# A later convolution beside a recurrent scan, and part of its loads issued by ScalarE

## The reference

```
x = x + conv(x, taps=cond) + conv_b          # per channel, causal, 128 taps over 64 steps
h = cond
for t in range(64):
    i_r, i_z, i_n = split(x[:, t] @ W_ih + b_ih)
    h_r, h_z, h_n = split(h @ W_hh + b_hh)
    r, z = sigmoid(i_r + h_r), sigmoid(i_z + h_z)
    n = tanh(i_n + r * h_n)
    h = (1 - z) * n + z * h
    out[:, t] = x[:, t] + h
```

## Time and profile before

| | |
|---|---|
| timed runs, median of 3 | 1212.7 us (1211.54 to 1214.32) |
| the profiled execution | 1213.68 us, of which 1211.9 us are the span of its instructions |
| PE busy | 1179.8 us, 97% of the span |
| DVE, ACT busy | 558.5 us (46%), 466.6 us (39%) |
| DMA packets | 251906, of these 176810 under 512 bytes |
| mean granted clock of TensorE | 0.995 of full speed |

### The profile page before, as it was taken

How to read it: one execution, slowest core, us unless ns; L and a number is a source line. 1 busy time by engine, 2 the same in 40 slices (tenths; PEclk the granted TensorE clock), 3 DMA queues, 4 the chain that set the end, 5 groups by cost and what they waited for, 6 DMA issues and landing times.

```text
span 1211.9 us, 14952 instructions
## 1 busy us (share of the span) xinstructions
PE 1179.8 (97%) x5524; PEld 977.4 (81%) x5524; DVE 558.5 (46%) x942; ACT 466.6 (39%) x804; POOL 15.0 (1%) x20
## 2 busy tenths in 40 slices
PE   5989999989999999999999999999999999999997
PEld 4968878878888888888888888888888888888886
DVE  3737768766874434334333343333433334333333
ACT  4346656656663333233332333332333323333232
POOL 0300000000000000000000000000000000000000
PEclk9989999999999999999999999999999999999999
DMA  9978888788842011110111101111011110011100
GB/s 260 284 144 165 164 171 170 160 171 178 165 124 70 20 34 35 35 35 20 32 35 35 35 21 31 35 35 35 22 30 35 35 35 24 28 35 35 35 18 18
DMA packets 251906, 92.18 MB, mean 76 GB/s; under 512 B 176810, under 2 KB 246442, under 8 KB 249824
## 3 DMA queue, kind: packets, MB, share of 16 engines
q1 hardware_dynamic: 248332, 90.52, 32.3%
q10 hardware_dynamic: 3540, 1.22, 0.4%
HBM read 57.56 MB, written 34.14 MB: 76 GB/s over the span
## 4 chain that ended last, share of the span: by engine, by line
PE 91%; SPq 3%; DMA 3%; DVE 1%; ACT 1%; issue 0%; ACTq 0%; DVEq 0%
PE bank L818 82%; PE bank L841 3%; PE bank L807 2%; PE bank L773 2%; SPq L361 1%; DMA xres<-stage 1%; PE bank L842 1%; DMA early<-early_result 1%; SPq L372 1%; PE bank L794 1%; SPq L346 1%; DMA conv_b_rows<-in_L_cond_b_dram 0%; DMA x_unit<-in_x_dram 0%; SPq L417 0%; DMA h<-in_cond_dram 0%
## 5 line engine op out<-in xcount | busy, mean ns | idle before, releaser
L818 PE MATMUL bank<-w_ih_hi,xT_hi 128*128 128x512 f32 x768 | 309.2, 403 | 1.7 <-ACT bank L546 1.7
L818 PE MATMUL bank<-w_hh_hi,hT_hi 128*128 128x512 f32 x768 | 304.4, 396 | 0.0
L818 PE MATMUL bank<-w_hh_hi,hT_lo 128*128 128x512 f32 x768 | 300.6, 391 | 0.0
L818 PE MATMUL bank<-w_hh_lo,hT_hi 128*128 128x512 f32 x768 | 300.4, 391 | 0.0
L818 PE MATMUL bank<-w_ih_hi,xT_lo 128*128 128x512 f32 x768 | 300.3, 391 | 0.0
L818 PE MATMUL bank<-w_ih_lo,xT_hi 128*128 128x512 f32 x768 | 299.5, 390 | 0.0
L818 PEld LDWEIGHTS bank<-w_hh_hi,hT_lo 128*128 128x128 f32 x768 | 144.9, 189 | 31.3
L818 PEld LDWEIGHTS bank<-w_ih_hi,xT_lo 128*128 128x128 f32 x768 | 144.2, 188 | 31.8
L818 PEld LDWEIGHTS bank<-w_ih_hi,xT_hi 128*128 128x128 f32 x768 | 144.4, 188 | 28.8 <-ACT bank L546 1.5
L818 PEld LDWEIGHTS bank<-w_hh_lo,hT_hi 128*128 128x128 f32 x768 | 145.0, 189 | 28.0
L818 PEld LDWEIGHTS bank<-w_hh_hi,hT_hi 128*128 128x128 f32 x768 | 144.9, 189 | 28.1
(11 more groups left out here) (68 smaller groups left out, 888.9 us busy)
## 6 DMA issues: line engine op xcount, KB each, us to landing
x_unit<-in_x_dram SPq DMA_DIRECT2D x64, 256.0 KB, 4.5
out_dram<-outZ SPq DMA_DIRECT2D x256, 64.0 KB, 1.6
toep_ring<-kernel_parts SPq DMA_DIRECT2D x128, 96.0 KB, 2.9
xres<-stage SPq DMA_DIRECT2D x32, 384.0 KB, 4.5
xT<-xres SPq DMA_DIRECT2D x48, 256.0 KB, 2.7
early<-early_result SPq DMA_DIRECT2D x4, 1024.0 KB, 16.3
xT<-early SPq DMA_DIRECT2D x60, 64.0 KB, 1.9
w_ih_raw<-in_L_cond_W_ih_dram SPq DMA_DIRECT2D x12, 256.0 KB, 8.5
```

The source lines that it names most:

```text
L818: mm = nc.tensor.matmul(psum[:, :], a[:, rows], b[w][:, cols], start=False, stop=stop and n == 2, skip_group_check=True)
```

## The change

The bulk moves from steps 1 to 13 to steps 2 to 14. The loads of early tiles 5 to 15 are issued by ACT in steps 2 to 12, each behind a wait for the previous step's `outT` and ahead of the split at point 4, and no more by SP in `finish`; tiles 1 to 4 stay with SP. In the last bulk step SP stores the last stage buffer, waits for all stage stores and loads steps 16 and 17 ahead of the step's own output store; the load of step 18 follows behind that. The helper `load_early_xT` stays the same but for the engine that issues; the last lines of the diff are in ACT's `step`.

```
-BULK_FIRST, BULK_LAST = 1, 13
+BULK_FIRST, BULK_LAST = 2, 14
...
+        def load_early_xT(eng, t):
+            for q4 in range(QUADS):
+                eng.dma_start(
+                    xT[t % RING][q4 * QUAD:(q4 + 1) * QUAD, :].rearrange("r (k b) -> r k b", b=B),
+                    early.rearrange("(q u h) (l r) b -> q u r (h l) b", q=QUADS, u=EARLY, r=QUAD)[
+                        q4, EARLY - 1 - t],
+                ).then_inc(xT_loaded[t % RING], 16)
...
             def finish(t):
                 sp.wait_ge(outZ_ready, t + 1)
                 store_out(t % RING, t)
-                if t + RING < EARLY:
-                    load_early_xT(t + RING)
...
+                if isinstance(t, int) and t == BULK_LAST:
+                    store_stage(NBANK * 2 // STAGE - 1)
+                    for n in range(2):
+                        sp.wait_ge(stage_stored[n], 32 * (PAIRS // STAGE // 2))
+                    for late in range(EARLY, t + RING):
+                        load_xT(late % RING, T - 1 - late)
                 if not isinstance(t, int) or t + 1 < BULK_FIRST or t >= BULK_LAST:
                     sp.wait_ge(outZ_ready, t + 1)
                     store_out(u, t)
...
                     if t == BULK_LAST:
-                        store_stage(NBANK * 2 // STAGE - 1)
-                        for n in range(2):
-                            sp.wait_ge(stage_stored[n], 32 * (PAIRS // STAGE // 2))
-                        for late in range(EARLY, t + RING + 1):
-                            load_xT(late % RING, T - 1 - late)
+                        load_xT(u, T - 1 - RING - t)
...
                     put_bias(ps_hn, bias_hn[:, :], bias_hn_put)
+                if isinstance(t, int) and BULK_FIRST <= t <= EARLY - RING:
+                    act.wait_ge(outT_ready, t)
+                    load_early_xT(act, t - 1 + RING)
                 split(split_block(t, 4))
```

More of the change, by code:

```diff
@@ L342, in _ @@
                              quarter[n][:, :]).then_inc(early_stored[n], 16)
[L344 to L350, removed]
             def load_xT(u, back):
@@ L388, in _ @@
             for t in range(1, RING):
-                load_early_xT(t)
+                load_early_xT(sp, t)
             sp.wait_ge(early_done, NB0)
@@ L438, in step @@
                     if t + RING < EARLY and t + 1 < BULK_FIRST:
-                        load_early_xT(t + RING)
+                        load_early_xT(sp, t + RING)
                     if t == BULK_LAST:
-                        store_stage(NBANK * 2 // STAGE - 1)
-                        for n in range(2):
-                            sp.wait_ge(stage_stored[n], 32 * (PAIRS // STAGE // 2))
-                        for late in range(EARLY, t + RING + 1):
-                            load_xT(late % RING, T - 1 - late)
+                        load_xT(u, T - 1 - RING - t)
                     if t > BULK_LAST and t + RING < T:
```

## The result

The changed kernel takes 1198.3 us (median of 4 runs, 1197.2 to 1199.8) beside 1213.5 us for the kernel before: a ratio of 0.9876 with a 95% interval of 0.9855 to 0.9898, 15.2 us less. The forecast was 1196.3 with a range of 1193 to 1206.

What follows compares the result with a forecast made beforehand. PE bounds the kernel (91% of the chain), with 17.8 us excess from its waits and lower clock; 17.8 - 1.1 - 0.3 = 16.4 us off, 1212.7 - 16.4 = 1196.3 us, less than 2 in 10 outside 1193 to 1206.

Steps and rivals of the forecast that it cites:

- The bulk one step later: First bulk step: PE's wait at bank 0 for the split of x and its lower clock go, 8.12 us gained.
- SP relieved: Later bulk steps: early tiles off SP end PE's eviction waits on stage stores, 4.06 + 4.70 + 0.90 us gained.
- rival B: SP's long issues are DMA waits, so moving early tiles gives nothing back: about 1201 us, chance 0.12.
- first stall: Bulk step of 25.51 us, PE idle 2.25 us at 181.12 for an eviction behind a stage store: 4.06 us excess.
- the 38.0 us for 16 banks: SP's time between stage stores from 136.54 to 174.57, against PE's 34.3 us: SP falls behind.
- Early tiles on ACT: Four issues ahead of the split at point 4 delay it 1.2 us, inside 1.5 us of slack before point 7.
- uneven steps: Allowance for ACT's issues in the bulk: 0.1 us a step, 1.1 us lost in all.
- The rule behind it: Each step loses ACT's total issue time less 1.06 us hidden and 1.5 us of slack.
- The end: After the last bulk step: r's bank ready at +11.0, x of step 16 wanted at +11.4; 0.3 us allowed.
- the likeliest case: Whole kernel: the forecast holds, 1194 to 1198.5 us, chance 0.62.
- A: ACT is held while issuing ahead of point 4's split: 1202 to 1212 us in part (0.10), 1241 at 1.68 each; in full 0.08.
- C: Step 16's load lands 1 to 3 us longer, holding ACT before step 15's sigmoid, then PE: 1197 to 1201 us, chance 0.08.

Runs made afterwards that it cites:

- ACT's issues alone: Kernel before the change, bulk kept in steps 1 to 13, but ACT issues early tiles 4 to 15 in steps 1 to 12: 1206.9 us, ratio 0.9943.
- The shift alone: Changed kernel, bulk in steps 2 to 14 and new order at its end, but SP issues the early tiles again: 1202.7 us, ratio 0.991 to before.
- eight issues a tile: Changed kernel, but ACT issues each early tile as eight DMAs of half the size instead of four: 1219.5 us, ratio 1.005 to before.

## Why the prediction was right, and what was off

**The bulk one step later: right.** The step without bulk was 16.79 us, the first with bulk 20.51 (worked out: 16.81 and 20.52); all 8.12 us went. The experiment with ACT's issues alone keeps them.

**SP relieved: right.** All of the 4.06 + 4.70 + 0.90 us are gone in the changed kernel. The stage stores themselves land no sooner (at the median 4.6 us behind their issue, 4.5 before), so it is their earlier issue that counts. The shift alone brings 3.8 us of them, where the text of rival B gave the whole first stall (4.06) to the start; in truth all three waits come back smaller. One reading behind this part was too strong: the 38.0 us for 16 banks hold 2.6 us in which SP waited for PE, so that its own work was about 35.4 us against PE's 34.3. SP came to its first duty in the bulk at 108.91, as worked out (about 107, in a scan that here began 1.77 us later), and waited 2.5 us for PE among the first ten Toeplitz blocks: it had no backlog.

**Early tiles on ACT: the size was right, the reason for the loss was not.** I allowed 1.1 us for uneven steps. It was 1.78 and 1.18 us in two executions, and it sits in one or two steps in which the issues were held, not spread over eleven. That 1.1 us came so near is luck in part. The delay worked out for a normal group (1.2 us) was 0.9 us: 1.93 instead of 1.06 us from bias to split. The rule behind it (PE loses the issue time less 2.56 us) gives 4.13 - 2.56 = 1.57 us for the long group against 1.50 measured, and 1.53 against 1.46 with eight issues.

**The end: right, without loss.** Ready at +10.8 instead of +11.0, needed at +11.4; the allowance of 0.3 us was not used. The tightness was real: a load issued 4.1 us later cost 3.58 us of waiting.

**The sum.** The profiled execution is 14.3 us faster than that of before: 17.8 less 1.78 in the two steps less 1.77 us ahead of the scan, where the last part of x for the early convolution landed 12.4 us after its issue in this execution and 10.3 us in that of before, and PE's first product with it begins at 24.52 instead of 22.43. Run once more, the changed kernel gave 1197.6, 16.3 us below the kernel before on that chip, as forecast (16.4). The first result, 15.2 us less, is a little short of that; 1198.3 us still lies at the upper end of the likeliest case (1194 to 1198.5). What the sum had no term for is the spread ahead of the scan, which was up to 2 us from run to run.

**The rivals.** A happens in one or two of eleven steps. The Trainium skill ("Perfetto Trace Analysis", "DMA Instruction — HWDGE (DVE, Sync)") has an issue wait for a generator locked by the other issuer; in the changed kernel nine of ACT's eleven groups took 1.8 to 2.2 us while SP was issuing, and the four from 192.20 on, of 0.31 to 0.63 us, ended inside a single issue of SP (191.00 to 194.50), against it. The long group of 256.56 is no such wait either: SP's store issues ended at 257.05 and SP issued nothing more until 263.05, while ACT's issues lasted until 260.69. Where both issuers were held behind a stage store, they came free within 0.01 us of each other (the last section shows the place); by the rule one would follow the other. B is refuted by the shift alone: its waits for a store are gone once ACT issues the tiles. C is refuted for the changed kernel, and its price was measured with the old order.

## What to carry to other kernels

Cut the time axis at a landmark of each iteration and subtract what the bottleneck engine needs for itself: here that gave the gain to within some 1 to 2 us. When a full issuing queue is relieved by another engine, put the issues where that engine idles or on an engine that does nothing, since their time is uneven; here that was worth another 1.8 us. And moving work later in a pipeline needs the order at its far end checked, where the slack of a whole step had shrunk to half a microsecond.

## What the runs showed of the hardware that was not expected

An issue of ACT that normally takes 0.45 us took up to 2.03 us. Of the 13 issues over 0.8 us in three runs (the changed kernel, ACT's issues alone, eight issues a tile) 11 lay within 3.5 us behind the second issue of a stage store (two DMAs of 384 KB), one 1.3 us behind a load of a unit of x, one behind neither. SP and ACT with eight issues a tile:

```profile
291.69 1.06 SPq L392 DMA_DIRECT2D xres<-stage  x2
292.80 2.13 SPq L381 DMA_DIRECT2D toep_ring<-kernel_parts  x1
```

```profile
292.89 2.03 ACTq L320 DMA_DIRECT2D xT<-early  x1
```

Both engines' next issues behind the store, for different queues and of different data, took 2.1 and 2.0 us side by side. They ended at 294.93 and 294.92. With the store cut to a sixteenth, one such hold was gone. What the two share there the traces don't show.

With eight issues a tile PE idled 3.31 us up to 300.51, and the granted clock of the step behind it stayed at 1.00:

```profile
300.51 0.36 PE L853 MATMUL bank<-x_parts,toep_ring 128*96 128x256 f32 x1 [3.31 <-DVE stage L722]
...
300.99:324.51 23.52, 21.70 (x119) 17.98 (x117) 16.36 (x35) 13.62 (x24) 0.00 (x0) 1.00 0.68 140
```

The shorter idle of 3.16 us one step earlier was followed by a clock of 0.50 (275.50 to 277.00, shown with that experiment), and so was the idle of 2.25 us in the kernel before, whose step has 0.93 in the mean. In this case the length of an idle alone doesn't tell whether it costs clock. The clock falls behind the wait, so a window that ends just after a wait shows it in the next one.
